# Alternating the score buffer in PSUM for the maxima of the first batch

## The reference

```python
w = jnp.floor(MIN_W + (MAX_W - MIN_W) * scale).astype(jnp.int32)   # 24 to 120
half = w // 2
scores = jnp.einsum('bhqd,bhkd->bhqk', q, k) * inv_sqrt
band = jnp.abs(idx[:, None] - idx[None, :]) <= half
scores = jnp.where(band[None, None], scores, -1e+30)
attn = jax.nn.softmax(scores, axis=-1)
out = jnp.einsum('bhqk,bhkd->bhqd', attn, v)
...
x = x + attention(_layernorm(x))
x = x + experts(_layernorm(x))        # gate softmax, top 2 of 8, W1, W3, silu, W2, Wf
```

## Time and profile before

| | |
|---|---|
| median of 3 runs | 1512.9 us (1511.43 to 1518.19) |
| the profiled execution's own time | 1508.1 us |
| its span in the trace | 1506.3 us |
| busy: PE, DVE, ACT, POOL | 1270.5, 968.7, 798.4, 647.7 us |
| first and last reduction of the maxima start at | 105.5 us, 851.0 us |

### The profile page before, as it was taken

The page is one execution under the profiler, slowest core; times in us unless marked ns, Lnnn a source line. Parts: engine busy times, 40 slices in busy tenths (PEclk is TensorE's granted clock), DMA queues, the critical chain, the costliest instruction groups (busy, mean ns, idle before and its releaser), DMA issues. The chain is left out here.

```text
span 1506.3 us, 46512 instructions
## 1 busy us (share of the span) xinstructions
PE 1270.5 (84%) x18200; PEld 930.1 (62%) x18200; DVE 968.7 (64%) x2064; ACT 798.4 (53%) x1388; POOL 647.7 (43%) x682
## 2 busy tenths in 40 slices
PE   6667888888788878887887773699999999999996
PEld 5534455554445545544555442588888888888885
DVE  4224668777776686778756656366666666666664
ACT  1344756666456655664554530355555555555554
POOL 2031422535345435354543645254455545544445
PEclk9867998998888888989987765799999999999999
DMA  6455464654545545545463232446654475464543
GB/s 130 166 130 145 99 188 102 174 128 127 161 127 142 149 105 173 132 122 162 113 171 98 88 99 85 106 66 122 126 113 66 66 175 69 64 123 67 66 64 48
DMA packets 226026, 175.35 MB, mean 116 GB/s; under 512 B 129082, under 2 KB 193082, under 8 KB 225866
## 3 DMA queue, kind: packets, MB, share of 16 engines
q1 hardware_dynamic: 167050, 116.62, 31.5%
q0 software_dynamic: 25728, 33.78, 13.0%
q10 hardware_dynamic: 33088, 22.71, 5.7%
HBM read 66.32 MB, written 89.40 MB: 103 GB/s over the span
## 5 line engine op out<-in xcount | busy, mean ns | idle before, releaser
L977 DVE TENSOR_REDUCE mx<-p_max 128x4 f32<-128x736 f32 (+1 forms) x256 | 219.1, 856 | 183.5 <-PE p_max L1248 179.2
L811 ACT ACTIVATE probs<-p_exp,unscale 128x736 f32<-128x736 f32 (+1 forms) x256 | 210.1, 821 | 206.3 <-PE p_exp L1248 204.4
L1491 PE MATMUL p_h<-xt_parts,w_hi 128*128 128x256 f16 x1824 | 273.7, 273 | 1.9 <-DVE xt_parts L1579 1.9
L1583 DVE SCALAR_TENSOR_TENSOR t<-p_h,b,t 128x256 f32<-128x256 f32 x272 | 131.0, 484 | 159.0 <-ACT t L1530 155.0
L1628 POOL DMA_INDIRECT out<-yw,tokens x136 | 211.9, 1558 | 28.3 <-POOL tick L1627 18.4
L1530 ACT ACTIVATE t<-p_h,b,undo 128x256 f32<-128x256 f32 x272 | 149.0, 559 | 91.8 <-PE p_h L1491 86.1
L1627 POOL TENSOR_TENSOR tick<-tick 128x1 f32<-128x1 f32 x136 | 82.9, 610 | 265.5 <-ACT yw L1547 265.5
L1491 PEld LDWEIGHTS p_h<-xt_parts,w_hi 128*128 128x128 f16 x1824 | 178.3, 98 | 22.7 <-DVE t L1583 2.1
L1491 PE MATMUL p_h<-xt_parts,w_lo 128*128 128x256 f16 x912 | 174.0, 273 | 0.0
L1241 PE MATMUL p_max<-mask,ident_bf 64*64 64x368 bf16 (+1 forms) x1024 | 93.8, 356 | 89.3 <-DVE mx L977 87.7
L706 POOL DMA_INDIRECT routed<-rows,slots x128 | 128.9, 1007 | 47.7 <-issue 47.7
(11 more groups left out here) (240 smaller groups left out, 2697.9 us busy)
## 6 DMA issues: line engine op xcount, KB each, us to landing
qk_dram<-qk_hi SPq DMA_DIRECT2D x128, 128.0 KB, 2.6
qs<-qk_dram SPq DMA_DIRECT2D x64, 192.0 KB, 4.2
ks<-qk_dram SPq DMA_DIRECT2D x64, 192.0 KB, 4.7
x_in<-in_x SPq DMA_DIRECT2D x64, 128.0 KB, 3.2
qk_dram<-qk_lo SPq DMA_DIRECT2D x64, 128.0 KB, 2.7
w_mat<-in_W ACTq DMA_DIRECT2D x32, 256.0 KB, 4.4
out<-x_sb SPq DMA_DIRECT2D x64, 128.0 KB
w_split<-w_first_hi SPq DMA_DIRECT2D x24, 256.0 KB
```

Of the source, the lines that this page charges most:

```text
L811: nc.scalar.activation(probs[r % 3][:, :, 0:hi - lo].rearrange("p (e s) w -> p e s w", e=2), p_exp[:, :, 0:2 * WIN].rearrange("p e (s w) - ...
L977: nc.vector.tensor_reduce(out=maxes, in_=p_max[:, :, 0:2 * WIN].rearrange("p e (s w) -> p e s w", s=2)[:, :, :, 0:hi - lo], axis=AX.X, op= ...
L1491: last = nc.tensor.matmul(p_h[:, m % KC, k, :], w[e][a][:, k, HID * c + P * m:HID * c + P * m + P], xt[:, x, c, :], start=(n == 0 and c == ...
L1583: nc.vector.scalar_tensor_tensor(t3[m // 2][:, m % 2, :], p_h[:, m % KC, 1, :], kept["b13"][:, 1, e, m:m + 1], t1[m][:], ALU.add, ALU.mult ...
```

## The change

For the 16 rounds of batch 0 the scores go to `p_max` and `p_exp` in turn: odd rounds to `p_exp`. PE then waits only for the reduction of the round before the last one. Round 16, the first of batch 1, goes to `p_max` and waits for round 14, the last one there; from round 17 on all is as before. The first exponentials of a batch get one more wait, for the 16 reductions of batch 0.

```diff
+def max_buffer(r, p_max, p_exp):
+
+    return p_exp if r < ROUNDS and r % 2 else p_max
...
-                nc.vector.tensor_reduce(out=maxes, in_=p_max[:, :, 0:2 * WIN].rearrange("p e (s w) -> p e s w", s=2)[:, :, :, 0:hi - lo],
+                nc.vector.tensor_reduce(out=maxes, in_=max_buffer(r, p_max, p_exp)[:, :, 0:2 * WIN].rearrange("p e (s w) -> p e s w", s=2)[:, :, :, 0:hi - lo],
                                         axis=AX.X, op=ALU.max).then_inc(s_mx, 1)
...
-                wait(pe, s_mx, r)
-                masked_scores(p_max, n, qs[b % 2], ks[b % 2], 3 * HD).then_inc(s_sc, 1)
+                wait(pe, s_mx, r - 1 if r <= ROUNDS else r)
+                masked_scores(max_buffer(r, p_max, p_exp), n, qs[b % 2], ks[b % 2], 3 * HD).then_inc(s_sc, 1)
...
             def score_for_exp(b, n):
                 if n == 0:
                     pe.wait_ge(s_mrow, 16 * MROW_DMAS * (b + 1))
+                    wait(pe, s_mx, ROUNDS)
```

## The result

| | before | changed |
|---|---|---|
| median time | 1511.49 us (20 runs) | 1502.72 us (20 runs) |
| ratio | | 0.9952, 95% interval 0.9933 to 0.997 |
| profiled execution: time, span | 1508.1, 1506.3 us | 1498.8, 1497.0 us |
| round 0 to the first scores for exponentials | 39.45 us | 31.82 us |
| first and last reduction of the maxima | 105.5, 851.0 us | 106.3, 840.2 us |

The change makes the kernel 0.5% faster. Single runs of either kernel spread over more than that (1501.3 to 1518.2 before, 1497.4 to 1519.0 changed), so one run tells nothing. The measured median is inside the forecast range.

A forecast was written before the change was run, and what follows sets the result against it. PE and DVE, with one buffer between them, were taken to wait for each other in the first stretch. Lost waits 7.2 plus clock 0.7 made 7.9 us, so 1512.9 - 7.9 = 1505.0 us, range 1499 to 1511.5.

The forecast's parts named there:

- the lost waits: Rounds 0 to 15: PE and DVE stop waiting for each other; gains of 2.2, 1.7, 1.4 and 1.9, sum 7.2 us.
- the clock: First pass: a denser pass may get more of the 2.4 GHz level; 0.7 us added to the gain.
- (a): Rival: the clock frees itself fully; gain 9 to 10.5 us, 1502.4 to 1503.9 us; chance 0.13.
- (b): Rival: lower clock in the pass, or weights and rows of maxima late; gain 2 to 5 us; chance 0.17.
- item (1): Transposes of batch 2: normalisation and values' bank ready about 112 us, PE there about 113.5; not binding unless values run at full clock.
- a gain of about 4: First pass: by the skill page's rule on cycling PSUM banks, the 0.7 us and more would be lost.
- Item (2): Round 16: stacked q and k of batch 1 land at 125.6 us, PE comes at 130.0; slack 4 us.
- Item (4): First exponentials: rows of maxima move by the same 7 us, but SP must first issue batch 2's staging; slack small but positive.
- its sign on the last reduction: End of the reductions: the last starts near 843 us instead of 851 if right, at 849 or later if wrong.
- Item (3): Fourth projection: ACT squares the first expert's weights from 133 to 135.2 us, projection done at 136.8; slack 1.6 us.
- Rival (c): Following steps: the shift is given back to other waits, SP's order or a load; gain under 2 us; chance 0.1.
- Rival (d): 146 to 851 us: slower as mean clock falls; gain gone from 0.012, 1521 us at 0.024; chance 0.05.

The follow-up runs named there:

- Experiment 2: The kernel before plus dummy scores (the filler) on PE behind nine rounds of batch 0, its waits between PE and DVE kept; ratio 0.999.
- experiments 8 to 10: The kernel before, unchanged, profiled three more times; stretches 37.19, 39.46 and 39.56 us, ratio of the first 0.9991.
- experiment 4: The changed kernel with the first expert's weights loaded later, in slot 12 of step -1 instead of slots 4, 6 and 10; ratio 0.9979.
- experiments 4 to 7: Four variants of the changed kernel: experiment 4; load of x for batch 3 ahead of batch 1's first staging, ratio 0.9969; experiment 6; experiment 7.
- experiment 6: The changed kernel with the DMAs of batch 0's rows of maxima ahead of the staging of batch 2 in SP's queue, step -1 alone; ratio 0.9949.
- experiments 3 and 4: First, the changed kernel with buffers in turn in rounds 0 to 3 alone, ratio 0.9961; second, experiment 4.
- experiment 1: The changed kernel measured again, unedited, against the kernel before; ratio 0.9951.
- experiment 7: The changed kernel with batch 3's load of x ahead of batch 1's first staging, and rows of maxima ahead of batch 2's staging; ratio 0.9948.
- experiment 11: The changed kernel with three moves in SP's queue: both of experiment 7, and batch 4's load of x behind batch 2's staging; ratio 0.9925.

## Why the prediction was right or wrong

**The sum.** Forecast a gain of 7.9 us, 1505.0 us and a range of 1499 to 1511.5; measured 1502.72 us, 8.8 us under before. At the first scores for exponentials the profiles show 39.45 - 31.82 = 7.6 us. The main mechanism, the lost waits, was right in kind and size. That the whole sum came out is luck: the clock gave about 5 us more than its term, and two waits that had been given slack took about as much back. In terms of the rivals, (a) and the late transfers of (b) both came true and cancelled; the measured time lies within the times of (a).

**The lost waits: right, near 7.2.** Rounds 0 to 3: 5.04 - 2.46 = 2.6 (forecast 2.2). Round 5 to the first projection: 6.01 against 116.78 - 111.70 = 5.08, so 0.9 (forecast 1.7); the transposes stood 0.58 us for the bank that ACT empties, the item (1) that I had dismissed on the ground that the values run slowly. Round 10 to the second projection: 1.9 (1.4). Round 13 to the third: 2.4 (1.9). Together 7.8. The second one was short for the cause that the prediction named and did not apply; the others were larger because PE's clock was higher than I let it be: a long round that waits takes 1.54 us at the full level and 1.86 at the lower one, and by that some 1.5 us of the 7.8 are the clock's (an estimate, for rounds 3, 10 and 13 to 15).

**The clock: sized far too small.** The 0.7 us in the sum were 5.3, beside the 1.5 just named: the values and rounds 4 and 5 took 3.37 instead of 5.60 us, and the three projections up to round 16, without the wait, 1.4 us each, 3.1 less in all. The forecast gave this case 0.13 as rival (a). Experiment 2 shows that the clock of the stretch needs no other cause than a busier PE, and experiments 8 to 10 that the old pass loses it each time. The row of the sparse and the slow stretch said as much, and the mistake was to go by a small part of it. The Trainium skill's rule in "TensorE: Matmul & The Clock Gate", Part 1, that activity releases the clock, agrees with experiment 2 (4.0 to 6.4 us). That page of the Trainium skill also tells of a kernel in which cycling through PSUM banks left PE idle in small pieces and let the clock swing (A second HAM failure mode). Here the buffers used in turn made these pieces shorter (0.78 to 1.03 us before rounds 1 to 3 became 0, 0.46 and 0.32), and the granted clock stayed at 1.00 from 105 to 125 us; so what the prediction drew from that page, a gain of about 4, did not come.

**What is late next: named, and called slack.** Item (2) had 4 us of slack for the stack of k: with the clock at 2.4 GHz, PE was ready for round 16 at 124.9 instead of 130.0, and the stack was late: PE could go on at 127.8, not at the 125.6 of the forecast. Of these 2.2 us, 0.8 are the later start of the whole pass (105.87 against 105.07), 0.6 the later issue and 0.9 the longer landing. The last of the weights were issued at 121.78 us instead of 130.48, and without them the wait was gone (experiment 4). Item (4), the rows of maxima, was called small but positive; it was -2.8 us. Together they took 5.7 us, about the 4.6 that the clock gave beyond its term. The forecast said that an idle PE for the rows of maxima, or an idle ACT ahead of L856, would prove it wrong, and both showed (2.83 and 2.08 us), while its sign on the last reduction (843; measured 840.2) and the one on the first exponentials (136 to 138; 137.69) came true. Item (3), ACT's squares, came with that wait of 2 us and did not delay the scaling of the fourth projection, for which ACT then waited 1.19 us on PE.

**Rival (c), given back later.** For the change itself it did not come; for the shorter stretches it did in part. Count from the first reduction (number 0) to number 63, the last one of batch 3. That takes 157.7, 157.1, 157.7 and 158.4 us in the kernel before, 150.9 and 149.6 in the changed one, 151.4 with the filler, 151.7 with rounds 0 to 3 alone, 150.9, 149.4, 148.5 and 149.1 in experiments 4 to 7, and 148.6 with the three moves. So the change is worth 7 us three batches on (and 11.7 us, 733.8 instead of 745.5, at the last reduction of the first two profiles), and the filler nearly as much. The three moves are worth only 1 to 2 us more than the change, though their stretch was 6 us shorter, and no more than experiment 6 with a stretch of 29.59 us: there, part was given back. From the first scores for exponentials to number 63 they take 123.5 us, where the changed kernel takes 119.6. In that time PE waits more for ACT and is granted less of the clock (the changed kernel first, then the three moves):

```profile
PE p_exp L1246 <- ACT probs L816: 3.8, 7, 1.8
137.70:257.30 119.60, 101.77 (x2203) 60.95 (x2204) 80.52 (x163) 78.21 (x111) 33.62 (x29) 0.92 0.47 122
```
```profile
PE p_exp L1253 <- ACT probs L823: 6.1, 8, 2.2
130.70:254.20 123.50, 104.30 (x2186) 61.42 (x2186) 81.14 (x163) 81.28 (x119) 34.73 (x30) 0.89 0.52 129
```

From number 63 to the last reduction the order of the work is the same in all these kernels, and yet the profiles of one chip differ: 612.8 us in the changed kernel, 619.1 with the filler, 615.8 and 613.5 in experiments 3 and 4. Why the filler's time is no shorter (0.999, to 0.996 at its interval's end, where 6.3 us would be 0.996) can't be settled with this scatter, and so it is not shown either how the 8.8 us of the whole time divide between lost waits and clock.

**Rival (d)**, a slower kernel, needed a fall of the clock of 0.012 in the long stretch. It fell by 0.01 in the profiles, and the stretch from the first exponentials' scores to the last reduction was no longer for it (702.5 against 706.5 us).

## What to carry to other kernels

In this kernel a ping-pong between two engines cost its waits and also the clock: price the TensorE work between the waits at both of its levels, and where a sparse stretch stands ahead of a slow one, give the faster level a large share of the chance. When an edit brings a stretch forward by more than the slack of a transfer, subtract that slack with the engine at its fastest, and count the transfers that move into the same stretch with it. What the second buffer won of the stretch in 16 rounds could be had almost whole from the first four, since the same transfer ended both. Moving three entries in a queue beside it took as much as 6 us more off the stretch (31.8 or 31.2 to 25.6 us), but only 1 to 2 us of that were left three batches on: follow a gain past the stretch in which it was made before you count it.

## What the runs showed of the hardware

Landing time grew with what else was moved: the stack of k was issued at 120.77 us in the changed kernel, took 5.9 us in the median against 5.0 before, and PE went on 7.0 us after its issue began. With the weights loaded later it landed in 4.1 us (experiment 4), against 5.4 in experiment 1. Four DMAs of 4 KB took up to 5.5 us from the issue at 139.01 to PE's start before, when the DMA share fell to 0.03, 6.0 us in the changed kernel with a share of 1.08 around the issue, 7.0 us from 125.75 in experiment 7 with 1.05, and 4.8 us from 125.92 in experiment 11 with 0.71. The small transfers were late where large ones filled the DMA engines.

Gaps of PE of 0.8 to 1.0 us in rounds of 1.2 to 1.9 us went with a granted clock of 0.70 to 0.79 over 105 to 138 us in four profiles of the kernel before; with dummy matmuls in the same gaps, which left 0.34 to 0.44 us of idle time in each, it was 1.00.
